# A mixture of experts from dense products to routed tiles of 128 rows, in a four-layer decoder kernel

## The chip, the cores and the metric

The kernel runs on one core of one Trainium2 chip. The metric is the time of one execution on the device, in microseconds. The core has TensorE (PE), VectorE (DVE), ScalarE (ACT), GpSimd (Pool), SyncE (SP, here a queue of transfers) and 16 DMA engines. All of them read their own instruction stream in order and wait for each other by semaphores.

## What is computed

A decoder with four layers on x of 4 batches x 256 tokens x 128 features, float32. Each layer adds a self-attention, a cross-attention to a context of 4 x 512 x 128, and a feed-forward part. Layer 0's feed-forward part is the one that changes:

```python
def _L0_ffn_ref(x, w_router, W1, b1, W2, b2, Ws1, bs1, Ws2, bs2):   # x = layernorm of the stream
    D_MODEL, D_FF, N_EXPERTS, TOP_K, N_SHARED = (128, 512, 8, 2, 1)
    SCALE = 1.0 / math.sqrt(N_SHARED + TOP_K / N_EXPERTS)
    logits = jnp.einsum('btd,ed->bte', x, w_router)
    probs = jax.nn.softmax(logits, axis=-1)
    vals, idx = jax.lax.top_k(probs, TOP_K)
    gates = jnp.sum(jax.nn.one_hot(idx, N_EXPERTS, dtype=x.dtype) * vals[..., None], axis=-2)
    hs = jax.nn.gelu(jnp.einsum('btd,fd->btf', x, Ws1) + bs1)
    acc = jnp.einsum('btf,df->btd', hs, Ws2) + bs2
    h = jax.nn.gelu(jnp.einsum('btd,efd->btef', x, W1) + b1)
    y = jnp.einsum('btef,edf->bted', h, W2) + b2
    acc = acc + jnp.einsum('bted,bte->btd', y, gates)
    return SCALE * acc
```

Every token has two chosen experts of eight, and a shared expert beside them. Layers 1 to 3 follow; layer 1 begins with an attention in hyperbolic form (`L1a`).

## The kernel before

It is one fully unrolled program: each engine has a Python function that writes its instructions in order, and the functions walk the same list of steps. Tokens are eight tiles of 128 (`NT`), tile t with its tokens on the partitions; `x` holds the stream, `xn` the normalised tokens, `xnT` the same turned, features on the partitions. A group g is four tiles, two batches of 256.

Cross-attention of layer 0 (`X0`) runs in slots (`cross_slot`); a slot up to 63 makes scores, slots 20 to 83 exponentials, and the last batch closes up to slot 95. Slot 66 holds the router's products for group 0 (`route`), DVE follows with `route_first` and `route_rest`, which find the two highest of eight. From slot 86 on the mixture's first products stand between the slots (`GELU_BEFORE`).

The mixture (`l0_mixture`) is dense. A unit u is a pair of group and expert, 9 experts (eight and the shared one) x 2 groups. For each unit PE makes four up-projections (`gelu_up`, 128 hidden rows x 512 tokens each, into the banks h0 and h1 in turn), ACT applies gelu with the bias of the hidden row (`gelu`), PE makes 16 down-projections per unit (`down`, four hidden parts for each of four token tiles, into banks e0 and e1), and DVE adds the result times the gate to x (`add_down`; an expert that isn't chosen has gate 0). The weights of all nine experts lie in `ffn_w`, 4.6 MB, loaded long before. Ups run two units ahead of downs. The gated sum of the biases b2 comes from `turn_gates` and `gated_bias`.

While group 1 is in the mixture, group 0 already enters layer 1: `l1_early(q)`, q from 0 to 35, are small pieces (norm turned, projection, the hyperbolic map on DVE with square root and exponentials on ACT, rows turned, query and key parts through DRAM into the stacks, then the nearest products `l1_near` and `l1_roots` of the first two units). Two of them stand at every half unit of group 1. After the mixture `l1_attention` goes on with batches 2 and 3 (`l1_take`) and eight units.

Pool makes the last step of each norm (`root`), and splits and sums of the attentions; SP issues nearly all transfers in one order (`self_attention_inputs` writes query and key parts and reads them back as stacks). An SP wait stops all transfers behind it.

Of the kernel before, what the change touches and what calls it, by code (L numbers as in the profile page):

```python
# [31 lines left out]
P = 128  # L32
# [21 lines left out]
NE = 8  # L54
# [8 lines left out]
HALF_STEPS = float(3 << 21)  # L63
BELOW_ONE = 1.0 - 2.0 ** -23
# [137 lines left out]
F2_HID0 = 108  # L202
F2_UP0 = 144
# [39 lines left out]
def build(nc, d, out, ctx):  # L243
# [44 lines left out]
    cm = sb("cm", [P, NT])  # L288

# [30 lines left out]
    def rows_by_head(tile):  # L320
# [22 lines left out]
                for part in (ffn_w[:, ROOM_AT + 3072:ROOM_AT + 5120], wk(4096, 2048))]  # L343
# [13 lines left out]
    pts[X1] = pts[X2] = pts[X0]  # L357
    gatesT = parts[:].rearrange("p s t -> p (s t)").bitcast(F32)[0:NE + 1, 0:TOK]
# [13 lines left out]
    v_scr = nc.dram_tensor("v_scr", (P, NC * VA), F32)  # L372

    (d_x, d_ident, d_keep, d_l0a, d_ctx, d_bf, d_rows, d_b2, d_ones, d_mrow, d_raw,
     d_cwrite, d_kxwrite, d_lam, d_cfill, d_vload, d_mask3, d_w, d_w1, d_w2, d_w3, d_out) = (
        semaphore("dma_" + n) for n in (
            "x", "ident", "keep", "l0a", "ctx", "bf", "rows", "b2", "ones", "mrow", "raw",
            "cwrite", "kxwrite", "lam", "cfill", "vload", "mask3", "w", "w1", "w2", "w3", "out"))
# [17 lines left out]
    rope_k, mask_row, vx_set = semaphore("rope_k"), semaphore("mask_row"), semaphore("vx_set")  # L396
    ctx_ps, ctx_done, gram_ps, gram_done, ctx_bias, c_split, kx_split, far_done, farT_ps, farT_done = (
        semaphore(n) for n in ("ctx_ps", "ctx_done", "gram_ps", "gram_done", "ctx_bias", "c_split", "kx_split",
# [13 lines left out]
    l1_pool_sq = semaphore("l1_pool_squared")  # L412
# [5 lines left out]
    UP0, HID0, DOWN0, BIAS0 = ({"L0f": 0, "L1f": 72, "L3f": 0}, {"L0f": 0, "L1f": 72, "L3f": 0},  # L418
                               {"L0f": 0, "L1f": 36, "L3f": 36 + L1F_UNITS}, {"L0f": 0, "L3f": 2})
    EXPERTS = {"L0f": NE + 1, "L1f": NE + 1, "L3f": NE}  # L420
    ROUTE_AT = {"L0f": 1, "L1f": 3, "L3f": 5}
    UPS, HIDS = {"L0f": up_ps, "L1f": up_ps, "L3f": up3_ps}, {"L0f": hidden, "L1f": hidden, "L3f": hidden3}

    def w1_of(st, e, j):
        if st == "L0f":
            return ffn_w[:, (e * FJ + j) * P:(e * FJ + j + 1) * P]
        if e < L3F_OWN:
            return ffn_w[:, (e * FJ + j) * P:(e * FJ + j + 1) * P]
        return ctx_flat[:, ((e - L3F_OWN) * FJ + j) * P:((e - L3F_OWN) * FJ + j + 1) * P]

    def w2_of(st, e, j):
        at = (e * FJ + j) * E
        if st == "L0f":
            return ffn_w[:, 9 * FH + at:9 * FH + at + E]
# [11 lines left out]
    def x_ready(st, b):  # L446
        if st == "L0a":
            return d_x, 16
        if st in ("L1a", "L2a"):
            ffn = "L0f" if st == "L1a" else "L1f"  # L450
            return down_x, down_at(ffn, EXPERTS[ffn] - 1, b)
        before = {"L0x": "L0a", "L0f": "L0x", "L1x": "L1a", "L1f": "L1x", "L2x": "L2a", "L2f": "L2x",
                  "L3a": "L2f", "L3x": "L3a", "L3f": "L3x"}[st]
        return x_done, X_AT[before, b]

# [38 lines left out]
    def route_tmp(i):  # L494
        flat = parts[:].rearrange("p s t -> p (s t)").bitcast(F32)
        return flat[:, TOK + i * NT * NE:TOK + (i + 1) * NT * NE].rearrange("p (t e) -> p t e", e=NE)

# [38 lines left out]
    def tensor_program():  # L536
# [304 lines left out]
        def turn_gates(st, n, g, routed):  # L841
            pe.wait_ge(gated, routed)
            claim("e1")
            for i in range(4):
                m = pe.transpose(ps_e[1][0:n, i * P:(i + 1) * P], gates[:, 4 * g + i, 0:n], ident)
            m.then_inc(gate_ps, 1)
            free["e1"] = (gate_T, BIAS0[st] + g + 1)

        def gated_bias(st, which, n, g):
            count = BIAS0[st] + g + 1  # L850
            claim("e0")
            pe.wait_ge(gate_T, count)
            for i in range(4):
                t = 4 * g + i
                m = pe.matmul(ps_e[0][:, i * P:(i + 1) * P], gatesT[0:n, t * P:(t + 1) * P], b2[0:n, which, :],
                              start=True, stop=True)
            m.then_inc(bias_ps, 1)
            free["e0"] = (bias_x, count)
# [23 lines left out]

        def l0_mixture():
            n_exp = NE + 1
            done = 0
            for t in range(TAILX, LAST[X0]):
                if t == min(GELU_BEFORE):
# [2233 lines left out]
```

## Time and profile before

| | |
|---|---|
| median of 3 runs | 1241.89 us (1233.96 to 1242.09) |
| span of the profiled execution | 1242.7 us |
| its difference to the median | 0.8 us more |
| instructions | 19890 |
| PE busy | 1039.3 us (84%) |
| DVE busy | 795.0 us (64%) |
| ACT busy | 611.8 us (49%) |
| Pool busy | 252.3 us (20%) |

The span runs from the first instruction to the last of one execution; no other time of that execution is known. Busy times are sums over stages with different limits, so a share says little about one stage: what matters is which engine is full in the stretch that a change touches, and what the others wait for there. A matmul in float32 shows as two records on PE, each with its own weight load (PEld). The granted clock is that of TensorE as a part of 2.4 GHz.

### The profile page before, as it was taken

The page shows a single profiled execution, that of the slowest core. Times are in us where ns is not written, and L with a number is a line of the kernel's source. Part 1 is how long each engine was busy: PE and PEld are TensorE (multiplying, and loading weights), DVE is VectorE, ACT ScalarE, POOL GpSimd, SP SyncE. Part 2 cuts the span into 40 slices and gives each one's busy share as a digit, 9 for nine tenths or more (in the row PEclk, how much of TensorE's full clock was granted, in tenths as well). Part 3 has the DMA queues.
Part 4 walks back from the last instruction along what each step waited for, and adds up shares of the span by engine and source line. Part 5 has one row for each costly group of instructions (what it writes and reads, how often), then busy time and mean ns, then how long its engine had stood idle before and what let it go on. Part 6 is the DMA issues. An engine that isn't in the chain of part 4 may idle for free.

```text
span 1242.7 us, 19890 instructions
## 1 busy us (share of the span) xinstructions
PE 1039.3 (84%) x7649; PEld 556.7 (45%) x7649; DVE 795.0 (64%) x1984; ACT 611.8 (49%) x1018; POOL 252.3 (20%) x309
## 2 busy tenths in 40 slices
PE   5777699999899975788877889999658878869999
PEld 4233223333677652355542333566323334437757
DVE  7786867731315468887767883777687886575412
ACT  2456356666334437678753777323125555333342
POOL 2933400000000225577641000001131001000000
PEclk9789879999999986566765999999867888779999
DMA  8332140000000300077014202600102100000000
GB/s 303 95 89 69 39 167 2 2 2 1 1 1 1 102 35 1 1 216 143 1 45 141 101 2 36 109 1 3 49 26 72 59 1 2 34 1 1 1 9 9
DMA packets 34786, 61.25 MB, mean 49 GB/s; under 512 B 4771, under 2 KB 25076, under 8 KB 33092
## 3 DMA queue, kind: packets, MB, share of 16 engines
q1 hardware_dynamic: 33828, 58.64, 16.5%
q8 instruction: 62, 1.02, 0.3%
q10 hardware_dynamic: 864, 1.33, 0.3%
q14 instruction: 32, 0.26, 0.1%
HBM read 42.91 MB, written 16.65 MB: 48 GB/s over the span
## 4 chain that ended last, share of the span: by engine, by line
PE 62%; DVE 27%; ACT 5%; issue 4%; DMA 1%; POOL 1%; SPq 0%; DVEq 0%; ACTq 0%; POOLq 0%
PE ps_s L879 10%; PE ps_e L869 9%; PE ps_v L672 7%; DVE mx L1864 5%; PE ps_e L608 5%; PE ps_s L629 3%; PE ps_e L606 3%; PE ps_e L973 2%; DVE ps_s L1860 2%; DVE mx L1854 2%; PE ps_s L960 2%; ACT work L1396 2%; PE ps_s L1124 1%; PE ps_v L1144 1%; DVE work L2339 1%
## 5 line engine op out<-in xcount | busy, mean ns | idle before, releaser
L1396 ACT ACTIVATE work<-ps_e 128x512 f32<-128x512 f32 x448 | 250.7, 598 | 144.3 <-PE ps_e L608 139.1
L2618 POOL TENSOR_TENSOR rstd<-rstd,halves 128x2 f32<-128x2 f32 x52 | 36.6, 705 | 699.5 <-DVE rstd L1807 699.4
L1864 DVE TENSOR_REDUCE mx<-ps_s 128x2 f32<-128x1024 f32 x128 | 154.0, 1222 | 30.0 <-PE ps_s L629 28.5
L629 PE MATMUL ps_s<-ctx_stack,q_stack 49*128 49x512 bf16 (+1 forms) x384 | 129.0, 452 | 46.0 <-DVE mx L1864 33.7
L1498 ACT ACTIVATE work<-ps_s,keep 128x512 f32<-128x512 f32 x136 | 93.0, 687 | 140.3 <-PE ps_s L879 137.3
L608 PE MATMUL ps_e<-q_stack,ctx_stack 52*128 52x256 bf16 (+1 forms) x768 | 151.4, 298 | 9.1 <-ACT work L1396 3.6
L672 PE MATMUL ps_v<-work,vaug 128*32 128x256 f32 x1536 | 132.4, 421 | 4.6 <-ACT work L1384 4.6
L869 PEld LDWEIGHTS ps_e<-ffn_w,work 128*128 128x128 f32 x960 | 118.9, 197 | 21.6 <-issue 20.5
L879 PE MATMUL ps_s<-xnT,ffn_w 128*128 128x512 f32 x240 | 118.4, 617 | 3.6 <-ACT work L1498 3.6
L869 PE MATMUL ps_e<-ffn_w,work 128*128 128x128 f32 x960 | 120.7, 281 | 0.8 <-DVE x L2050 0.8
L2060 DVE SCALAR_TENSOR_TENSOR x<-ps_e,gates,x 128x128 f32<-128x128 f32 x128 | 38.9, 346 | 123.4 <-PE ps_e L869 120.3
L1860 DVE CUSTOM_DVE_ANT_0 ps_s<-ps_s,work 128x512 f32<-128x512 f32 x128 | 86.0, 717 | 29.1 <-PE ps_s L629 29.1
L608 PEld LDWEIGHTS ps_e<-q_stack,ctx_stack 52*128 52x128 bf16 (+1 forms) x768 | 45.0, 97 | 105.2 <-ACT work L1396 49.5
L629 PEld LDWEIGHTS ps_s<-ctx_stack,q_stack 49*128 49x128 bf16 (+1 forms) x384 | 29.6, 97 | 72.2 <-DVE mx L1864 46.7
L879 PEld LDWEIGHTS ps_s<-xnT,ffn_w 128*128 128x128 f32 x240 | 41.7, 195 | 41.9 <-issue 25.3
L672 PEld LDWEIGHTS ps_v<-work,vaug 128*32 128x32 f32 x1536 | 31.7, 112 | 49.8 <-issue 36.7
L606 PE MATMUL ps_e<-work,ident_b 128*128 128x512 bf16 x128 | 51.8, 404 | 2.3 <-issue 2.3
L2677 POOL TENSOR_TENSOR work<-work 128x1536 f32<-128x1536 f32 x14 | 47.9, 3441 | 0.9 <-ACT work L1642 0.8
L1376 ACT ACTIVATE xnT<-ps_m 128x256 f32<-128x256 f32 x36 | 13.7, 382 | 61.9 <-PE ps_m L554 60.1
L1854 DVE TENSOR_REDUCE mx<-ps_s 128x4 f32<-128x1024 f32 x32 | 38.1, 1220 | 9.4 <-PE ps_s L624 9.1
L1895 DVE RECIPROCAL rsum<-ps_s 128x8 f32<-128x8 f32 x48 | 9.7, 203 | 48.9 <-PE ps_s L577 48.7
L577 PE MATMUL ps_s<-keep,work 128*128 128x128 f32 x128 | 29.3, 312 | 12.9 <-ACT work L1384 6.5
(379 smaller groups left out, 1821.5 us busy)
## 6 DMA issues: line engine op xcount, KB each, us to landing
q_stack<-q_scr SPq DMA_DIRECT2D x32, 192.0 KB
ffn_w<-in_L0f_w SPq DMA_DIRECT2D x1, 4608.0 KB, 15.9
ffn_w<-in_L1f_w SPq DMA_DIRECT2D x1, 3456.0 KB, 12.9
q_scr<-parts SPq DMA_DIRECT2D x16, 192.0 KB, 2.1
c_scr<-ffn_w SPq DMA_DIRECT2D x12, 256.0 KB, 7.1
kx_scr<-ffn_w SPq DMA_DIRECT2D x12, 256.0 KB, 4.1
ctx_stack<-kx_scr SPq DMA_DIRECT2D x2, 1536.0 KB
ctx_stack<-c_scr SPq DMA_DIRECT2D x2, 1536.0 KB
```

What stands on the lines that cost most here:

```text
L606: pe.matmul(bank[name], ident_b[:], far_k[:, b, k:k + 2, :].rearrange("p k q -> p (k q)"), start=True, stop=False, skip_group_check=True)
L608: m = pe.matmul(bank[name][:, half * S:(half + 1) * S], stack[p0:p0 + n_rows, pair, k * P:(k + 1) * P], q_stack[p0:p0 + n_rows, b, pair, : ...
L629: return pe.matmul(ps_s[i][:, parity, :], q_stack[p0:p0 + n_rows, b, pair, part * P:(part + 1) * P], ctx_stack[p0:p0 + n_rows, pair, b * S ...
L672: m = pe.matmul(ps_v[j * COLS:(j + 1) * COLS, 0:S], values(b * nkt + k, g % 4 * GROUP + j), pt[:, j % 2, k % 2, :], start=(k == 0), stop=( ...
L869: m = pe.matmul(bank[name][:, i * P:(i + 1) * P], hid[:, j, (t0 + i) * P:(t0 + i + 1) * P], w2(e, j), start=(j == 0), stop=(j == FJ - 1))
L879: pe.matmul(bank[name], w1_of(st, e, j), xnT[:, g * 512:(g + 1) * 512], start=True, stop=True).then_inc(UPS[st], 1)
L1396: act.activation(pt[:, parity, :, :].rearrange("p k q -> p (k q)"), bank[f"e{parity}"], ACT.Exp).then_inc(exped, 1)
L1498: act.activation(hid_unit(st, u)[:, j, :], bank[f"h{n % 2}"], ACT.Gelu_apprx_tanh, bias=b1).then_inc(HIDS[st], 1)
L1854: m = dve.tensor_reduce(mx[:, b, :, pair, :], ps_s[i][:].rearrange("p a (q k) -> p a q k", q=TPB), AX, ALU.max, negate=True)
L1860: m = dve.tensor_tensor_reduce(ps_s[i][:, parity, :], ps_s[i][:, parity, :], far_q[:, b * TPB + part, :], 1.0, -3e38, ALU.add, ALU.max, mx ...
L1864: m = dve.tensor_reduce(mx[:, b, :, pair, part], ps_s[i][:], AX, ALU.max, negate=True)
L2677: pool.tensor_tensor(c, c, l1_s[:, HALVES[n], :], ALU.add).then_inc(added, 1)
```

## The change

The dense mixture of layer 0 becomes a routed one.

- For each group of 512 tokens DVE takes the two chosen experts per token (`chosen`); PE counts with small products how many tokens come before each within an expert (`moe_rank`: a triangular matrix of 2^66 and a vector of it). DVE turns the counts into a row number for both choices of every token, each expert beginning at a multiple of 128, and from the same counts the expert of each tile of 128 rows (`moe_place`). 1024 rows with 8 experts fill at most 15 tiles; 15 are always computed (`SPARSE_TILES`).
- Pool scatters the 1024 rows to DRAM with eight indirect transfers per group (`send_rows`); SP loads them back in order (`rows_in`); PE turns the 15 tiles (`moe_turn`) and DVE copies them to `xgT`.
- 38 tile steps follow: 15 of group 0, 8 of all tokens with the shared expert, 15 of group 1. Each has four up-projections and four down-projections of 128 columns (`tile_rise`, `tile_fall`). The start column of each tile's expert is loaded into registers of PE and DVE (`moe_experts`, 15 registers each per group). DVE copies the expert's W1 into a ring of four buffers (`stage`), addressed by register; PE reads W2 in place, addressed by register. ACT makes four gelus of 128 columns per tile with biases picked by `moe_place`.
- The routed results go by groups of four tiles to SBUF (ACT), to DRAM (a store issued by ACT, `y_group`), and are fetched per token by eight indirect gathers per group on Pool (`take_y`). DVE adds them times the gate (`add_chosen`). The shared expert's results are added from PSUM (`add_shared`).
- The 36 early pieces of layer 1 stand at other places: 22 of them two to a tile in the last eleven tiles, 14 after the last tile.
- Beside that: DRAM scratch for both groups is filled once with rows of x by four transfers (so that unused rows hold numbers), the gate and bias products use banks m and v, and several semaphores are reused.

The diff, cut to its core:

```diff
-GELU_FIRST = [(u, j) for u in range(3) for j in range(FJ)]
-GELU_BEFORE = {87: 1, 88: 1, 89: 2, 90: 2, 91: 2, 92: 2, 93: 2}
 ROUTE0 = 66
-GATES1 = 3
+SPARSE_TILES = (2 * 4 * P + NE * (P - 1)) // P
+MOE_TILES = [(0, i) for i in range(SPARSE_TILES)] + [("all", t) for t in range(NT)] + [(1, i) for i in range(SPARSE_TILES)]
+MOE_BEFORE = {86: 1, 87: 1, 88: 1, 89: 1, 90: 1, 91: 1, 92: 1, 93: 1}
+MOE_RANK0, MOE_PLACE0, MOE_TURN0 = 69, 70, (82, 83, 84, 85)
+MOE_RANK1, MOE_GATES1, MOE_TURN1 = 10, 12, (21, 22, 24, 26)
+MOE_MIX0 = (25, 26)
+MOE_EARLY = {n: (2 * (n - 27), 2 * (n - 27) + 1) for n in range(27, 38)}
+MOE_RING = 4
...
+        def moe_experts(st, g):
+            pe.wait_ge(*planned(st, g, "experts"))
+            _, at = nc.values_load_multi_w_load_instructions(
+                expert_at[0:1, g, 0:SPARSE_TILES], engines=[mybir.EngineType.PE], min_val=0, max_val=(NE - 1) * FH,
...
+        def tile_rise(n):
...
+                pe.wait_ge(xg_T, XG_T0 + 4 * g + i // 4 + 1)
+                pe.wait_ge(staged, STAGED0 + MOE_STAGED.index(n) + 1)
+            for j in range(FJ):
+                if g == "all":
+                    w = ffn_w[:, (NE * FJ + j) * P:(NE * FJ + j + 1) * P]
+                else:
+                    w = w1_staged[MOE_STAGED.index(n) % MOE_RING][:, j * P:(j + 1) * P]
+                m = pe.matmul(bank[name][:, j * P:(j + 1) * P], w, rhs, start=True, stop=True)
+            m.then_inc(tile_up, 1)
+            free[name] = (tile_hidden, n + 1)
+
+        def tile_fall(n):
...
+            pe.wait_ge(tile_hidden, n + 1)
+            for j in range(FJ):
+                lo = 9 * FH + j * E
+                w = ffn_w[:, lo + NE * FH:lo + NE * FH + E] if g == "all" else ffn_w[:, bass.ds(expert_of[g][i] + lo, E)]
+                m = pe.matmul(bank[name][:, at:at + P], tile_hid[n % MOE_RING][:, j, :], w, start=j == 0, stop=j == FJ - 1)
+            m.then_inc(tile_down, 1)
+            free[name] = moe_group_done(k)
+
+        def moe_step(n):
...
+            if n in MOE_TURN1:
+                moe_turn(1, MOE_TURN1.index(n))
+            if n + 2 < len(MOE_TILES):
+                tile_rise(n + 2)
+            if n == MOE_STAGED[SPARSE_TILES]:
+                moe_experts("L0f", 1)
+            tile_fall(n)
+            for q in MOE_EARLY.get(n, ()):
+                l1_early(q)
...
+            for n in range(n, len(MOE_TILES)):
+                moe_step(n)
+            for q in range(2 * len(MOE_EARLY), 36):
+                l1_early(q)
...
+        def tile_gelu(n):
...
+            act.wait_ge(tile_up, n + 1)
+            for j in range(FJ):
+                bias = kp("L0f_bs1", j, 1) if g == "all" else hidden_bias[g][:, i * FJ + j:i * FJ + j + 1]
+                m = act.activation(tile_hid[n % MOE_RING][:, j, :], bank[moe_tile_bank(n)][:, j * P:(j + 1) * P],
+                                   ACT.Gelu_apprx_tanh, bias=bias)
+            m.then_inc(tile_hidden, 1)
...
+        def stage(n):
+            m = MOE_STAGED.index(n)
+            g, i = MOE_TILES[n]
+            if m >= MOE_RING:
+                dve.wait_ge(tile_up, MOE_STAGED[m - MOE_RING] + 1)
+            dve.tensor_copy(w1_staged[m % MOE_RING], ffn_w[:, bass.ds(expert_of[g][i], FH)]).then_inc(staged, 1)
...
+        def add_chosen(b):
+            g = b // 2
+            dve.wait_ge(moe_x, g + 1)
+            dve.wait_ge(d_y_own[b % 2], 64 * (g + 1))
+            for c in range(2):
+                for t in tiles(b):
+                    m = dve.scalar_tensor_tensor(x[:, t, :], y_own[g][:, t % 4, c, :], chosen_gate[:, c, t:t + 1],
+                                                 x[:, t, :], ALU.mult, ALU.add)
...
+        def send_rows(st, g):
...
+            pool.wait_ge(*planned(st, g, "placed"))
+            for c in range(2):
+                for t in range(4 * g, 4 * g + 4):
+                    pool.indirect_dma_start(rows_scr[g].ap()[:, :], bass.IndirectOffsetOnAxis(ap=place_of[:, c, t:t + 1], axis=0),
+                                            xn[:, t, :], None).then_inc(d_rows_out, 16)
+
+        def take_y(st, g):
+            pool.wait_ge(d_y_out[g], Y_OUT0[g] + 64)
+            for b in (2 * g, 2 * g + 1):
+                for t in tiles(b):
+                    for c in range(2):
+                        pool.indirect_dma_start(y_own[g][:, t % 4, c, :], None, y_scr[g].ap()[:, :],
+                                                bass.IndirectOffsetOnAxis(ap=place_of[:, c, t:t + 1], axis=0)
+                                                ).then_inc(d_y_own[b % 2], 16)
...
+        def rows_in(g):
+            sp.wait_ge(d_rows_out, 128 * (g + 1))
+            sp.dma_start(xg[g], rows_scr[g].rearrange("(t p) f -> p t f", p=P)).then_inc(d_rows_in, 16)
```

## Rows read from the trace of the kernel before

**Rows 1.** The page, 40 equal slices of the span, PE's busy tenths.

```profile
PE   5777699999899975788877889999658878869999
```

**Rows 2.** The page, the chain that ended last, shares of the span by engine.

```profile
PE 62%; DVE 27%; ACT 5%; issue 4%; DMA 1%; POOL 1%; SPq 0%; DVEq 0%; ACTq 0%; POOLq 0%
```

**Rows 3.** Busy time in stretches: PE, PEld, DVE, ACT, Pool, clock, DMA share, GB/s.

```profile
316.60:380.00 63.40, 61.69 (x345) 46.07 (x346) 14.65 (x55) 21.79 (x31) 0.00 (x0) 0.95 0.00 1
380.00:427.00 47.00, 45.35 (x256) 32.61 (x255) 25.45 (x82) 23.52 (x39) 9.44 (x18) 1.00 0.13 40
```

**Rows 4.** Timeline (start, length): first up, first down, a load, last down.

```profile
296.39 1.12 PE L879 MATMUL ps_s<-xnT,ffn_w 128*128 128x512 f32 x2
...
316.65 5.39 PE L869 MATMUL ps_e<-ffn_w,work 128*128 128x128 f32 x32 [0.78 <-DVE x L2050]
...
323.17 0.19 PEld L869 LDWEIGHTS ps_e<-ffn_w,work 128*128 128x128 f32 x1 [0.24 <-issue]
...
454.99 2.00 PE L869 MATMUL ps_e<-ffn_w,work 128*128 128x128 f32 x16
```

**Rows 5.** The chain that ended last, in order of time: start, length, what.

```profile
369.32 1.72 PE ps_s L879 x4
371.04 1.78 PE ps_e L869 x16
...
449.39 3.16 PE ps_e L869 x16
```

**Rows 6.** Timeline of the attention's end: last gate operation, exponentials, two transposes.

```profile
266.24 0.19 DVE L2038 TENSOR_TENSOR gates<-parts 128x32 f32<-128x32 f32 x1
...
290.92 1.24 ACT L1396 ACTIVATE work<-ps_e 128x512 f32<-128x512 f32 x2 [0.61 <-PE ps_e L608]
...
311.61 0.38 PE L554 MATMUL ps_m<-keep,xn 128*128 128x128 f32 x2
```

**Rows 7.** Groups of instructions by form: count, busy us, mean ns, idle before.

```profile
L2627 POOL TENSOR_TENSOR x<-x,rows 128x128 f32<-128x128 f32 x32 | 12.8, 421 | 10.3 <-DVE xn L1820 10.3
L2677 POOL TENSOR_TENSOR work<-work 128x1536 f32<-128x1536 f32 x14 | 47.9, 3441 | 0.9 <-ACT work L1642 0.8
L2020 DVE TENSOR_TENSOR parts<-parts 128x32 f32<-128x32 f32 x12 | 2.3, 193 | 0.4
L1860 DVE DVE_READ_ACCUMULATOR2_ANT mx<- 128x1 f32 x128 | 18.1, 141 | 0.0
L1498 ACT ACTIVATE work<-ps_s,keep 128x512 f32<-128x512 f32 x136 | 93.0, 687 | 140.3 <-PE ps_s L879 137.3
L1606 ACT ACTIVATE ctx_stack<-ctx_stack 128x128 f32<-128x128 f32 x2 | 0.6, 309 | 3.4 <-DVE ctx_stack L2258 3.4
L2237 DVE TENSOR_SCALAR work<-work 128x256 f32<-128x256 f32 x4 | 1.2, 289 | 0.1
L2237 DVE TENSOR_SCALAR work<-work 128x704 f32<-128x704 f32 x4 | 2.1, 527 | 0.1
L2239 DVE TENSOR_TENSOR work<-work 128x704 f32<-128x704 f32 x4 | 3.6, 893 | 0.1
```

**Rows 8.** DMA issues: times, KB each, median us from issue to landing.

```profile
q_scr<-parts SPq DMA_DIRECT2D x16, 192.0 KB, 2.1
```

**Rows 9.** Timeline of layer 1's start, first `l1_take` to the last two.

```profile
388.39 0.96 DVE L2311 TENSOR_TENSOR ctx_stack<-ps_s,rows 128x770 f32<-128x770 f32 x1 [0.69 <-PE ps_s L1060]
...
415.38 0.56 DVE L1830 TENSOR_TENSOR parts<-qT,parts 128x256 bf16<-128x256 f32 x1
415.97 1.46 SPq L2805 DMA_DIRECT2D q_scr<-parts  x3
...
427.61 0.34 PE L1073 MATMUL ps_s<-self_stack,q_stack 48*128 48x128 bf16 x4
...
458.77 0.68 DVE L2319 TENSOR_REDUCE mx<-ps_s 128x2 f32<-128x512 f32 x1
...
465.16 0.96 DVE L2311 TENSOR_TENSOR work<-ps_s,rows 128x770 f32<-128x770 f32 x1 [3.41 <-PE ps_s L1060]
```

More of the change, by code:

```diff
@@ L881, in gelu_up, with moe_rank @@
             free[name] = (HIDS[st], n + 1)
+        def moe_rank(st, g, name):
+            claim(name)
+            pe.wait_ge(*planned(st, g, "counted"))
+            ps = bank[name]
+            ones = ones_big[:].broadcast_to([P, P])
+            pe.matmul(ps[:, 0:4 * NE], far_b[:], chosen[:].rearrange("p t e -> p (t e)"), start=True, stop=False,
+                      skip_group_check=True)
+            for i in range(3):
+                pe.matmul(ps[:, (i + 1) * NE:4 * NE].rearrange("p (t e) -> p t e", e=NE), ones,
+                          chosen[:, i:i + 1, :].broadcast_to([P, 3 - i, NE]), start=False, stop=i == 2,
+                          skip_group_check=True)
+            for i in range(4):
+                m = pe.matmul(ps[:, 4 * NE:5 * NE], ones, chosen[:, i, :], start=i == 0, stop=i == 3,
+                              skip_group_check=True)
+            m.then_inc(ranked, 1)
+            free[name] = planned(st, g, "placed")
@@ L1501, in l0_mixture, with moe_step @@
+        def moe_step(n):
+            if n == -1:
+                tile_gelu(0)
+                tile_gelu(1)
+                return
+            if n + 2 < len(MOE_TILES):
+                tile_gelu(n + 2)
+            k = MOE_GROUP_OF[n]
+            if n == MOE_GROUPS[k][-1] and MOE_TILES[n][0] != "all":
+                y_group(k)
+            for q in MOE_EARLY.get(n, ()):
+                l1_early(q)
         def l0_mixture():
-            n_exp = NE + 1
-            done = 0
+            n = -1
@@ L1522, in l3_route @@
+            for q in range(2 * len(MOE_EARLY), 36):
+                l1_early(q)
         def l3_route(g):
@@ new lines, in moe_turn, with moe_experts @@
+        def moe_turn(g, k):
+            lo, hi = 4 * k * P, min(4 * k + 4, SPARSE_TILES) * P
+            if k == 0:
+                dve.wait_ge(*planned("L0f", g, "biases"))
+            dve.wait_ge(xg_ps, XG_PS0 + 4 * g + k + 1)
+            dve.tensor_copy(xgT[g][:, lo:hi], bank[moe_turn_bank(g, k)][:, 0:hi - lo]).then_inc(xg_T, 1)
+        def moe_experts(st, g):
+            dve.wait_ge(*planned(st, g, "experts"))
+            _, at = nc.values_load_multi_w_load_instructions(
+                expert_at[0:1, g, 0:SPARSE_TILES], engines=[mybir.EngineType.DVE], min_val=0, max_val=(NE - 1) * FH,
+                skip_runtime_bounds_check_because="the vector engine clamps it to the last expert")
+            expert_of[g] = at
@@ L2780, in gpsimd_program @@
         settle(pool.tensor_tensor(rw("L2a_bin"), rw("L2a_bin"), rw("L2a_gamma"), ALU.mult))
-        for b in range(B):
-            root("L0f", b)
+        root("L0f", 0)
+        root("L0f", 1)
+        send_rows("L0f", 0)
+        root("L0f", 2)
+        root("L0f", 3)
+        send_rows("L0f", 1)
+        take_y("L0f", 0)
         l1_attention()
@@ L2969, in sync_program @@
         sp.wait_ge(down_ps, down_at("L1f", NE, B - 1))
[L2970 removed]
+        sp.dma_start(ffn_w[:, 0:own], d["L3f_w"][:, 0:own]).then_inc(d_w1, 16)
         max_rows(X2, 2)
```

398 lines of the change are left out of this document (287 added, 111 removed).

## Prediction, made before the changed kernel ran

> **What bounds the kernel now.** I read the page first: PE is busy in nearly every slice [rows 1], and the chain that ended last runs through PE for 62% [rows 2]. The stretches around the change came next, with a granted clock of 0.95 and 1.00 [rows 3]. The dense mixture is PE's from 296.4 us, its first up-projection, to 457.0, where its last down-projection ends [rows 4]: PE is busy 61.7 of 63.4 us in the first half while ACT has 21.8 and DVE 14.7. From 380 the second half of the mixture runs beside the first steps of the next layer (`l1_early`), and PE still stays near full.
>
> The chain shows the pattern that a reader should keep: 1.72 us for two up-projections of 512 columns, 1.78 us for eight down-projections of 128, over and over [rows 5]. So an up costs 0.86 us and a 128-column matmul 0.223 us; at half clock eight cost 3.16 us.
>
> **Experts on PE.** Before: 18 units (nine experts, two groups) of 4 ups and 16 downs, 2 x (1.72 + 1.78) = 7.0 us each, 126 us. After: 38 tiles of 128 rows (15 per group, always, whatever the routing, and 8 for the shared expert) of 8 matmuls of 128 columns, 1.78 us each, 68 us. That is -58 us on an engine that sets the end. It is the only large credit; all else is a debit.
>
> **In front of the mixture.** The first group is planned inside the attention's last slots. DVE is nearly idle there and PE is full. DVE's gates are done at 266.4 us [rows 6]; one exponential step takes about 2 us of PE, so slot 69 begins near 266, and `moe_rank` may wait 1 us for `chosen`. Its 8 small matmuls cost about 1 us and the 15 transposes 2.3 us (0.11 to 0.19 each, from two in 0.38 [rows 6]). PE is the bound here, so all of it counts: +4.5 us. The ten short operations of `moe_place` ahead of the scatters take about 2.4 us (0.19 each and a gap), those behind 2.6 us [rows 7], and both lie in DVE's idle time.
>
> The eight scatters on Pool, then one load, must be done when slot 82 transposes, near 291 us [rows 6]. From 270.5 that leaves 20 us; less about 2.5 us for each landing (2.1 us for a small store [rows 8]) 15 remain, 1.8 us per scatter. No row shows an indirect transfer: the nearest are Pool's operation on 128x128 (0.42 us) and on 128x1536 (3.43 us) [rows 7]. I take 1.3 us, nearer the first because a scatter has 128 short pieces to describe, and then nothing waits; at 3.4 us this place alone would stall PE by 13 us.
>
> **Registers.** PE and DVE each load 15 start columns per group. No row has a register load; the nearest is DVE's read of an accumulator, 0.14 us [rows 7], hence 2.1 us per set, with ends of 0 and 0.5 us each (an issue on SP [rows 9]), 7.5 us per set. Exposed are DVE's first set (PE's first tile waits for it and for one staging copy) and both of PE's: +6.7 us. The first tiles also stand in the attention's tail: 16 half tiles of 0.89 are 14.3 us where 12 ups were 10.3. That moves work and is no cost by itself.
>
> The Trainium skill, Runtime: NRT & Kernel Launch, section on instruction fetch mechanics, gives about 200 ns per register for such loads, from HBM. By it a set would be 3 us and the sum 2.7 us worse; no run here shows it yet.
>
> **Per tile on the other engines.** ACT: a gelu of 512 columns takes 0.687 us with its per-row bias [rows 7], where a pair of exponentials of 512 without one takes 1.24 [rows 6]; a 128-column pass takes 0.309 us [rows 7]. So 128 columns with bias cost some 0.36, and back to back, as in that pair, down to 0.26. Four are 1.1 to 1.5 us, a quarter of a group's copy, wait and store issue 0.3: 1.4 to 1.8 us against PE's 1.78. It is hidden, barely; at its upper end it costs nothing, but 0.1 us more per tile would cost 4 us. DVE: the staging copy of 512 columns interpolates to 0.43 us between two one-input operations on SBUF, 0.289 for 256 columns and 0.527 for 704 [rows 7]. Hidden, and four tiles ahead.
>
> These one-input operations run at about twice the rate of the two-input ones (0.527 against 0.893 us for 704 columns [rows 7]). The Trainium skill, SBUF — State Buffer, Who interferes with whom, says that such a copy locks Pool out of the port by which it writes descriptors. It speaks against this change, whose staging copies run beside its scatters and gathers: each transfer would be held up to one copy, 0.43 us, and 1.3 would become 1.7. The sum above has room for that.
>
> **The second group.** Rank and 15 transposes +4 us on PE; gates and bias now sit in other banks than the tiles, so PE no longer waits for the addition to x before going on (-1). Scatters begin with `placed` near tile 11, the load must land by tile 21, about 21 us: 2 us per scatter are allowed. The gathers of group 0 follow on Pool and have till tile 25. Behind a late `add_chosen(0)` on DVE stand the staging copies, so lateness would stop PE.
>
> Without the next layer the sum is -58 + 4.5 + 6.7 + 4 - 1 = -44 us.
>
> **What the next layer gives back.** It is the step that a sum of PE time misses. In the kernel before 36 early pieces spread over 66 us of group 1. Now 22 of them stand two to a tile in the last 11 tiles (20 us of PE) and 14 behind the mixture. They form a chain through DVE, ACT with table loads, Pool and DMA. By my clock: before, the expert part of PE from its first down is at 316.65 us; after, tile 7 begins near 327. Twenty tiles (35.6), rank, gates, transposes and PE's registers (about 8.5) bring tile 27 to 371 and the first `l1_take` to 375, where before it was at 388.4. From there [rows 9]:
> - take to the end of the split: 27.6 us before, less three additions of downs (1.8), 25.7 -> 400.7;
> - to the first near product: 11.7 us before (two chained DMA steps with their issues), about 10 -> 410.7. PE has finished its tiles by 408, so these transfers lie bare;
> - 7 near and 4 root pieces up to the last reduction: 31.8 us before, with eight groups of downs between; without them PE 0.7, DVE 1.05 and 0.3 of hand-over per near, 2.35 per root, 23.5, plus 2 us because PE's clock may fall when its tiles are gone (it was half from 449 on [rows 5]) -> 436.2;
> - to the last `l1_take`: 5.7 us before; now two `add_chosen` and two norms, 3.8 us each, and 2.8 -> 446.6.
>
> The last gathers (store 3, eight gathers 10.4, landing 2 after the last tile at 408) are done at 423 and hidden behind the 14 pieces; uncovered they would cost 13. That take stood at 465.2 us [rows 9], so the layer starts 18.5 us earlier: of 44 us saved 25 are given back. The remaining layers are unchanged; the renamed semaphores and the 2 MB that fill the scratch rows early (DMA is near idle once the attention's slots have begun) cost nothing.
>
> Sum: 1242.7 - 18.5 = 1224.2 us by the profiled span. The median of the runs is 0.8 us lower than the span, so 1224 us. The three runs differ by 0.65%; 1%, 12.4 us, is about what a measurement here can tell from no change.
>
> **Rivals.**
> 1. PE pays for register-addressed matmuls. Each routed fall has four matmuls (eight records) whose moving operand is at a register, with an addition to form the address. In the trace PE's loads stand idle up to 0.24 us "issue" ahead of a group [rows 4]. If each such matmul costs that much more, a fall costs 0.96 more, 30 of them 29 us, some 5 hidden in the last tiles: 1248 us. Per record it would be 58 us, about 1270: slower. It decides from 0.14 us per record on, where the 18.5 and the 12.4 us are both used up. For it: a tile already has 32 PE instructions in 1.78 us. Against: at full clock those groups run at the pace of the data (0.11 us per record, and 0.2 at half clock [rows 5]), so the queue is not what binds now. The Trainium skill, TensorE: Matmul & The Clock Gate, Part 2, gives about 62 ns per matmul for one decoded in software; by it a record would still fit in 0.11 us, though not with two register additions.
> 2. Indirect transfers are slow, 2.5 us or more each. Group 0 waits 5.6 us, group 1 4, the gathers 5 and the tail 5, so 1224 + 18 = 1242 us: no change. Pool is one queue, and `l1_added_least` stands behind the last eight gathers.
> 3. The chain is looser than it looks: early pieces overlap as before, register loads cost nothing, 1205 to 1213 us. For it: DVE is busy only 25.5 of 47 us in that stretch [rows 3].
> 4. The change doesn't do what it says: 15 tiles always run, where 1024 rows fill 8 to 15; that is already counted.
>
> **How the numbers follow.** Forecast case (1212 to 1230) 0.40; rival 3 0.13; rival 1 in its lighter form 0.12, in its heavy form 0.15; rival 2 0.14; register loads or ACT's cadence at their upper ends (1230 to 1245) 0.06. Likeliest: 1224 us. Its own range is 1212 to 1234, from the 23.5 us piece (up to 31.8) and from faster hand-overs. For 8 in 10: 1205 to 1260. Faster by over 1% (below 1229.5): 0.48; within 1%: 0.27; slower (above 1254.3): 0.25.
>
> **What would show it.** Tiles of 1.8 us with PE full from tile 7 to 27; an attention tail 4 to 5 us longer; idle PE of 10 us or more around the first near product; the `l1_take` of the last batch near 447 us. Wrong if falls are visibly longer than rises, if PE waits for DVE's staging, if Pool's queue is solid from the first scatter on, or if PE's clock is half inside the tiles.

## The result, and the profile after

| | us | runs |
|---|---|---|
| before | 1242.4 (1233.5 to 1249.1) | 20 |
| after | 1248.3 (1240.7 to 1254.7) | 20 |
| forecast | 1224 (1205 to 1260) | |

The ratio is 1.005, 95% interval 1.0029 to 1.0072: slightly slower, where I had forecast 1.5% faster. The profiled execution of after took 1250.0 us, its span is 1248.3 (before: 1242.7). The time lies inside my range, but by luck: rival 1's 1248 is the nearest figure that I named, and its mechanism isn't what happened. The repeats below make the story unusual: on two other chips the same program took 1223.7 and 1227.6, on a third 1248.6.

First the page of after, PE's busy tenths and its granted clock by slice of 31.2 us, to be held against [rows 1].

```profile
PE   6777699999898524778877989999658868779999
PEclk9789879995888856556775999999867989879999
```

The clock of before by the same slices, and its windows around the tail of the attention (stretch, length, busy time of PE, PE's loads, DVE, ACT and GpSimd, then granted clock, DMA share and GB/s):

```profile
PEclk9789879999999986566765999999867888779999
```

```profile
280.00:290.00 10.00, 10.00 (x80) 3.36 (x76) 1.37 (x6) 6.67 (x13) 0.67 (x1) 1.00 0.01 2
290.00:300.00 10.00, 8.64 (x74) 2.67 (x66) 0.43 (x2) 5.87 (x10) 0.00 (x0) 1.00 0.01 2
300.00:310.00 10.00, 8.56 (x25) 3.67 (x26) 1.76 (x8) 5.39 (x10) 0.36 (x1) 1.00 0.00 0
```

The tiles themselves are what I priced. Two pieces of the chain that ended last (start, length, what), the rise (four up-projections) of one tile and the fall (four down-projections) of an earlier one:

```profile
327.80 0.89 PE ps_s L999 x8
328.69 0.89 PE ps_e L1013 x8
```

A fall takes its weights from an address in a register, the rise here from a fixed one, and both take 0.89 us, as the 1.78 us for sixteen records in [rows 5] promised. PE's busy time went from 1039.3 to 999.7 us, and to 985.9 in the same program on chip 6. So the gain is there, and it is lost elsewhere. These milestones say where (start times in us; "unchanged, chip 6" is the same program, experiment r1):

| | before | forecast | after | unchanged, chip 6 |
|---|---|---|---|---|
| first work of the experts on PE | 296.4 | 301 | 317.6 | 301.1 |
| first `l1_take` | 388.4 | 375 | 400.0 | 375.8 |
| first near product | 427.6 | 410.7 | 433.4 | 409.1 |
| third `l1_take` | 465.2 | 446.6 | 474.1 | 447.7 |
| end of the span | 1242.7 | 1224.2 | 1248.3 | 1227.2 |

Most of the loss is there before the first tile. The windows show why, with the columns of those above. Both fences are the attention's last slots, first after, then the same program on chip 6:

```profile
285.00:310.00 25.00, 25.00 (x113) 6.48 (x110) 2.06 (x7) 9.12 (x16) 0.12 (x1) 0.50 0.11 31
```

```profile
285.00:310.00 25.00, 20.20 (x170) 10.91 (x168) 5.79 (x14) 13.13 (x31) 0.00 (x0) 1.00 0.05 13
```

PE is full in after and does less: 113 matmul records where the other has 170. Its clock is at 1.2 GHz (0.50) through the tail, where it was 1.00 before the change (the windows of before above). What happened just before it fell is in the timeline of after:

```profile
277.55 0.44 PE L650 MATMUL ps_m<-keep,xn 128*128 128x128 f32 x2
...
279.10 0.64 PE L737 MATMUL ps_v<-work,vaug 128*32 128x256 f32 x8
279.14 0.96 POOL L3005 DMA_INDIRECT rows_scr<-xn,l0a_ss  x1 [0.30 <-issue]
279.90 0.38 ACT L1537 ACTIVATE qT<-ps_m 128x256 f32<-128x256 f32 x1 [2.21 <-remote]
...
280.40 0.96 POOL L3005 DMA_INDIRECT rows_scr<-xn,l0a_ss  x1 [0.30 <-issue]
280.43 0.68 PE L658 MATMUL ps_s<-keep,qT 128*128 128x128 f32 x4 [0.68 <-issue]
281.31 0.60 ACT L1545 ACTIVATE work<-ps_e 128x512 f32<-128x512 f32 x1 [1.03 <-issue]
...
281.96 0.39 PE L671 MATMUL ps_e<-work,ident_b 128*128 128x512 bf16 x1 [0.85 <-issue]
...
282.65 0.39 SPq L3191 DMA_DIRECT2D self_stack<-rows_scr  x1
...
282.88 0.42 DVE L2114 TENSOR_TENSOR x<-ps_s,x 128x256 f32<-128x256 f32 x1 [8.36 <-remote]
...
283.38 0.39 PE L671 MATMUL ps_e<-work,ident_b 128*128 128x512 bf16 x1 [0.71 <-ACT work L1545]
...
284.24 1.08 PE L737 MATMUL ps_v<-work,vaug 128*32 128x256 f32 x8
```

ACT needs only L650, which ended at 277.99, and starts at 279.90, 1.9 us late; DVE needs L658, over at 281.11, and starts at 282.88, 1.8 us late. The trace can tie neither start to an engine's signal ("remote"), so whether the signal or the engine itself is held isn't shown. PE has three gaps, 0.68, 0.85 and 0.71 us, and the clock falls behind the last: L737 takes 0.64 us at 279.10 and 1.08 at 284.24. All this falls beside the last two of the eight scatters and in the 2 us behind them. On chip 6 the same two instructions start 0.03 us after theirs:

```profile
276.21 0.44 PE L650 MATMUL ps_m<-keep,xn 128*128 128x128 f32 x2
...
276.68 0.38 ACT L1537 ACTIVATE qT<-ps_m 128x256 f32<-128x256 f32 x1 [0.34 <-PE ps_m L650]
...
278.33 0.71 PE L658 MATMUL ps_s<-keep,qT 128*128 128x128 f32 x4
...
279.07 0.42 DVE L2114 TENSOR_TENSOR x<-ps_s,x 128x256 f32<-128x256 f32 x1 [5.90 <-PE ps_s L658]
```

The same picture returns in after beside the gathers of group 0. DVE's copy needs the transposes that ended at 376.79 and starts 3.5 us later; PE waits 4.24 us for it, and its clock is down afterwards (0.70 over 380 to 390).

```profile
376.19 0.60 PE L973 MATMUL ps_v<-keep,ctx_stack 128*128 128x128 f32 x4
...
380.25 0.69 DVE L2262 COPY work<-ps_v 128x512 f32<-128x512 f32 x1 [4.20 <-remote]
380.58 0.94 POOL L3013 DMA_INDIRECT self_stack<-y_scr,l0a_ss  x1 [0.31 <-issue]
...
381.04 1.19 PE L999 MATMUL ps_s<-work 128*128 128x128 f32 x4 [4.24 <-issue]
```

### The profile page after: what moved, and what is told of

It reads as the page before. It is cut to its first block, busy times and chain, and to the rows that moved or that the text cites. A ratio compares the mean times of both kernels' runs of the same rounds, so it can differ in the third digit from the quotient of the medians.

```text
span 1248.3 us, 20081 instructions
## 1 busy us (share of the span) xinstructions
PE 999.7 (80%) x7583; PEld 543.1 (44%) x7583; DVE 806.5 (65%) x2007; ACT 609.0 (49%) x1106; POOL 284.2 (23%) x341
## 3 DMA queue, kind: packets, MB, share of 16 engines
q0 software_dynamic: 1024, 2.10, 0.6%
## 4 chain that ended last, share of the span: by engine, by line
PE 57%; DVE 29%; ACT 6%; issue 5%; DMA 2%; POOL 1%; SPq 0%; DVEq 0%; ACTq 0%; POOLq 0%
PE ps_v L737 7%; DVE mx L2040 6%; PE ps_e L673 5%; PE ps_s L946 5%; PE ps_e L936 4%; PE ps_s L694 3%; PE ps_e L671 3%; PE ps_s L999 3%; PE ps_e L1118 2%; DVE ps_s L2036 2%; DVE mx L2030 2%; PE ps_s L1105 2%; ACT work L1545 2%; PE ps_e L1013 2%; DVE work L2626 1%
## 5 line engine op out<-in xcount | busy, mean ns | idle before, releaser
L737 PE MATMUL ps_v<-work,vaug 128*32 128x256 f32 x1536 | 134.6, 427 | 4.3 <-ACT work L1533 4.3
L1644 ACT ACTIVATE work<-ps_s,keep 128x512 f32<-128x512 f32 x64 | 43.8, 687 | 68.0 <-PE ps_s L946 66.6
L2318 DVE SCALAR_TENSOR_TENSOR x<-ps_e,gates,x 128x128 f32<-128x128 f32 x64 | 19.4, 346 | 60.9 <-PE ps_e L936 58.0
L671 PE MATMUL ps_e<-work,ident_b 128*128 128x512 bf16 x128 | 55.0, 430 | 3.8 <-issue 3.1
L737 PEld LDWEIGHTS ps_v<-work,vaug 128*32 128x32 f32 x1536 | 31.8, 113 | 49.6 <-issue 35.6
L946 PE MATMUL ps_s<-xnT,ffn_w 128*128 128x512 f32 x96 | 50.8, 659 | 2.0 <-ACT work L1644 2.0
L1656 ACT ACTIVATE work<-ps_s,kv 128x128 f32<-128x128 f32 x120 | 34.0, 370 | 33.9 <-PE ps_s L999 33.8
L936 PEld LDWEIGHTS ps_e<-ffn_w,work 128*128 128x128 f32 x384 | 46.0, 192 | 7.8 <-issue 7.7
L936 PE MATMUL ps_e<-ffn_w,work 128*128 128x128 f32 x384 | 46.4, 275 | 0.0
L619 PE MATMUL ps_m<-keep,xn 128*128 128x128 f32 x80 | 19.8, 336 | 29.9 <-DVE xn L1996 28.4
L1013 PE MATMUL ps_e<-ffn_w,work 128*128 (+1 forms) x304 | 43.6, 291 | 0.0
```

The source lines that it names most:

```text
L671: pe.matmul(bank[name], ident_b[:], far_k[:, b, k:k + 2, :].rearrange("p k q -> p (k q)"), start=True, stop=False, skip_group_check=True)
L737: m = pe.matmul(ps_v[j * COLS:(j + 1) * COLS, 0:S], values(b * nkt + k, g % 4 * GROUP + j), pt[:, j % 2, k % 2, :], start=(k == 0), stop=( ...
L936: m = pe.matmul(bank[name][:, i * P:(i + 1) * P], hid[:, j, (t0 + i) * P:(t0 + i + 1) * P], w2(e, j), start=(j == 0), stop=(j == FJ - 1))
L946: pe.matmul(bank[name], w1_of(st, e, j), xnT[:, g * 512:(g + 1) * 512], start=True, stop=True).then_inc(UPS[st], 1)
L1013: m = pe.matmul(bank[name][:, at:at + P], tile_hid[n % MOE_RING][:, j, :], w, start=j == 0, stop=j == FJ - 1)
```

## Experiments

Theory 1: the indirect transfers hold up the other engines for some 2 to 4 us, PE idles, and its clock falls. The edits are against after. e1, e2, e9, e10, e12, e13 and e14 leave out the sorting of the rows by expert, and e4 the choice of the expert, so these eight don't compute the mixture; the number and size of their tiles are those of after.

**1. What carries the rows (e1, e2; chip 4).** `send_rows` and `take_y` (in e2 `send_rows` alone) leave GpSimd; SP sends plain transfers of the same size:

```diff
-        send_rows("L0f", 0)
-        send_rows("L0f", 1)
-        take_y("L0f", 0)
...
+                for t in range(4 * g, 4 * g + 4):
+                    lo = (4 * c + t % 4) * P
+                    sp.dma_start(rows_scr[g].ap()[lo:lo + P, :], xn[:, t, :]).then_inc(d_rows_out, 16)
```

> All 32 indirect transfers are replaced by plain transfers of the same bytes, pieces and semaphore counts from SP's queue, so tokens are not sorted by expert (that part of the computation is left out; tiles, weights, registers and adds stay). Theory 1 (the indirect transfers hold up PE, ACT and DVE for 1 to 3 us each time they run, PE's granted clock then falls to 1.2 GHz and stays there through the exponential tail): the clock stays 1.00 from 280 to 312, the first tile starts at 304 to 307 instead of 317.6, the stall at 377 to 381 is gone, and the kernel takes 1222 to 1232. Theory 2 (the clock falls because the ranking matmuls, the transposes and their waits were put into PE's order in the slots, whatever carries the rows): the clock falls at 283 as after, time 1244 to 1250.

> Only the 16 scatters are plain transfers from SP's queue; the 16 gathers stay indirect on GpSimd (rows are not sorted by expert, as said of the run with all 32). Theory 1: the clock's fall at 283 is gone with the scatters, the tail of the exponentials runs at 1.00, first tile at 304 to 307, but the stall at 377 beside the gathers and the odd waits at 433 to 441 stay; 1228 to 1238. Theory 2: as after, 1244 to 1250. If the time is that of the run with all 32 plain, the gathers cost nothing.

Measured: 1225.3 (ratio 0.984, interval 0.979 to 0.990) and 1221.0 (0.982, 0.977 to 0.987), clock 1.00 from 285 to 310 in both. e2 is below its own range of 1228 to 1238: the gathers cost nothing there. The rest looks like theory 1, until the next two are read.

**2. The wait for the gates, and the registers (e3, e4; chip 4).**

```diff
-MOE_RANK1, MOE_GATES1, MOE_TURN1 = 10, 12, (21, 22, 24, 26)
+MOE_RANK1, MOE_GATES1, MOE_TURN1 = 10, 14, (21, 22, 24, 26)
```

```diff
-            _, at = nc.values_load_multi_w_load_instructions(
...
+            expert_of[g] = [i // 2 * FH for i in range(SPARSE_TILES)]
```

> The second group's gate transposes and bias stand at step 14 instead of 12, so DVE has finished placing the second group before PE waits for its copy. Theory 1 counts this wait (354.8 to 357.3) and the half clock behind it (358 to 362) as 4 to 5 us that nothing later absorbs: 1242 to 1245. Rival (the path behind the mixture is set by the second group's scatters, their landing and the transposes, not by PE): the wait goes, but the last fall stays at 424 to 426 and the time at 1247 to 1249.

> The expert of each tile is a constant of the program (tile i takes expert i/2), no registers are loaded and no address is taken from one: the choice of the expert is left out, all else stays. My term of 2.1 us for a set of register loads: both sets shown as 1.8 us on DVE, of which the first is exposed, so 1 to 3 us less: 1245 to 1247. Rival 1 of the prediction (register-addressed matmuls are slow): falls shorter than 0.89 us and 15 or more us off the time, 1233 or less. The trace of after speaks against that: falls take 0.89 us, as the rises with fixed addresses do.

Measured: 1222.7 (0.986, 0.980 to 0.992) and 1221.9 (0.986, 0.981 to 0.990). e3 is 20 us below all that was expected of it and differs from after only from 350 us on, long after the damage. e4's time would suit rival 1 (1233 or less), but its falls, now with fixed addresses, take the same 0.89 us; by its other term it is 23 us too low. A result that no theory allows is a reason to repeat the base, not to explain.

**3. The unchanged kernel again, and two that barely differ (chip 6).** e5 has the gates at step 13, e6 one more memset at the start.

> The changed kernel once more, unchanged, on the chip of these runs. The run with the gates two steps later took 1222.7 although its program and its work are the same as after up to 350 us, and it shows none of after's stalls at 278 to 283. Theory 3 (the stalls beside the scatters belong to this program as it is loaded, or to its exact order): 1245 to 1252, with the scatters landing in a median of some 6 us and the first tile at 317. Theory 4 (they belonged to the runs shown, not to the kernel): about 1226 to 1229, the gates' move being worth 4 to 6 us.

> Second group's gates and bias at step 13 instead of 12 (14 took 1222.7). Up to 350 us nothing differs from after in what is computed or in its order. Theory 3 by the order behind 350: PE still waits a little for DVE here, and the time lies between 1223 and 1230. If the program's placement decides and not the order, the stalls at 278 to 283 may be back and the time 1240 to 1248.

> After with one memset of GpSimd more at the very start of the program (it writes a constant a second time, some 0.1 us where GpSimd is free), so that only the placement of GpSimd's instructions differs. Theory 3 by placement: the stalls at 278 to 283 go and the time falls to 1226 to 1230. Theory 3 by order: 1245 to 1252 as after. Theory 4: the same as the repeated after, whatever that is.

Measured: 1227.6 (0.987, 0.980 to 0.993), 1227.2 and 1224.5, all at a clock of 0.93 to 1.00 over 285 to 310, with no "remote" wait in it. Theory 4 (the stalls belonged to the runs shown, not to the kernel): neither order nor placement matters. One reading of mine has to be taken back here and in all expectations that repeat it: the "6.1 us" was the landing of other transfers to the same tensor. Of the scatters in after the trace shows no landing. They are not late: SP, which waits for all eight, issues its load 1.29 us after the last scatter's issue ended in after (281.36 to 282.65), and 1.28 us in r1 (280.02 to 281.30).

**4. A third repeat and an idle made by hand (chip 15).**

```diff
+            if t == OVERLAP + 75:
+                pe.wait_ge(d_rows_out, 128)
```

> The changed kernel unchanged, a third time. Repeated on another chip than that of the first experiments it took 1227.6, its scatters landed in a median of 2.2 us (6.1 us in the profile after) and its tail of exponentials ran at a granted clock of 1.00. If slow landings come with the chip or its state and not with the kernel, this one is either such a chip (landings of 6 us, half clock from 283 on, 1245 to 1252) or not (2.2 us, 1.00, 1224 to 1230); nothing between.

> After, and PE waits behind slot 75 of the cross-attention until the first group's 8 scatters have landed, so that it idles some 3 us at 279 to 282, where the profile after shows its idle. Theory 1, clock part (an idle of 2 to 3 us there takes the granted clock to 1.2 GHz for the whole tail of the exponentials): the clock reads 0.50 from about 283 to 310, the first tile comes 13 to 20 us later than in the unchanged kernel of the same chip, and the time is 12 to 18 us above it. Rival (the idle costs itself only, the clock fell for another reason): clock 1.00, 2 to 4 us more.

> The same wait one slot later, where only 1 to 1.5 us of idle are left. Theory 1: if the clock falls here too, the tail is as sensitive as that, and the time is again 12 to 18 us above the unchanged kernel; if it does not, the idle must be longer than that to cost the clock, and the time is 0 to 2 us above.

> The kernel with the second group's gates at step 14 again, to stand beside the unchanged one on one chip. It took 1222.7 where before took 1242.6, the unchanged one 1227.6 where before took 1243.3. The wait for DVE's copy is 2.0 us and the half clock behind it costs about 2.5 us in the repeated profile: 4 to 5 us below the unchanged one. If other waits absorb it: within 2 us.

Measured: 1248.6 (1.006, 1.003 to 1.009; 10 runs), 1246.9, 1250.2 and 1250.4. This chip does what the result showed: "remote" waits beside the scatters in all four, clock 0.50 to 0.55 over 285 to 310. The added waits change nothing, since PE idles there anyway. e3's kernel took 1222.7 on chip 4 and 1250.4 here, and before took 1242.6 and 1242.0. So the change has two values, by chip: I call chips like 4 and 6 the first sort, those like this one the second. On this chip the move of the gates gains nothing, 1250.4 against 1248.6, where 4 to 5 us were expected. In r1 PE waits for the copied gates, in e3 for a staged expert, which stands behind the same `moe_place(1)` on DVE:

```profile
338.85 1.12 PE L922 MATMUL ps_v<-b,parts 9*128 9x128 f32 x8 [1.99 <-DVE parts L2302]
```

```profile
340.06 1.13 PE L999 MATMUL ps_s<-self_stack,work 128*128 128x128 f32 x8 [1.82 <-DVE work L2276]
...
345.17 1.12 PE L922 MATMUL ps_v<-b,parts 9*128 9x128 f32 x8 [0.86 <-DVE parts L2302]
```

**5. Which transfers, on a chip of the second sort (chip 13).** e9 and e10 are the kernels e1 and e2; e11 is e7; in e12 GpSimd issues the 32 transfers with fixed rows:

```diff
-                    pool.indirect_dma_start(rows_scr[g].ap()[:, :], ...
+                    lo = (4 * c + t % 4) * P
+                    pool.dma_start(rows_scr[g].ap()[lo:lo + P, :], xn[:, t, :]).then_inc(d_rows_out, 16)
```

> All 32 indirect transfers plain from SP's queue (rows not sorted by expert), once more, in the hope of a chip on which the indirect scatters land in 6 us; the run with the wait at slot 75 shows which kind this one is. Theory 5 (on such a chip the software-described transfers hold up the other engines, and the 21 us between 1227.6 and 1248.5 are theirs): 1222 to 1230 whatever the chip. Rival (such a chip is slow for this kernel also without them, by its clock for instance): 1240 to 1250 where the kernel with them has 1248. On a chip with landings of 2.2 us: 1222 to 1230 by both.

> Only the 16 scatters plain, the gathers indirect. Theory 5 on a chip with slow landings: the first group's scatters cost 13 to 16 us by the lost clock of the tail of the exponentials, the gathers the rest: 1228 to 1236, first tile near 301 and clock 1.00 to 300. If the gathers do not matter: as with all plain.

> All 32 transfers issued by GpSimd as direct ones with fixed rows (not sorted by expert): same queue, bytes and pieces as the indirect ones, no row numbers. On a chip with slow landings, theory 5a (it is the software queue that holds the engines up): 1243 to 1250 as with indirect ones. Theory 5b (it is the row by row addressing): 1222 to 1230. On a chip with landings of 2.2 us it tells only what issuing costs GpSimd: within 3 us of the others.

> PE waits behind slot 75 for the first group's scatters to land. On the chip with slow landings it took 1246.9, as the unchanged kernel, whose PE idles there anyway. On a chip with landings of 2.2 us: theory 1's clock part gives a granted clock of 0.50 from about 283 to 310 and 1238 to 1246; without it 1228 to 1232.

| chip 13 | us | ratio, interval |
|---|---|---|
| e11, all indirect (and the wait) | 1251.6 | 1.007, 1.004 to 1.010 |
| e10, gathers indirect | 1234.9 | 0.993, 0.991 to 0.996 |
| e12, none, from GpSimd | 1226.8 | 0.988, 0.984 to 0.991 |
| e9, none, from SP | 1228.3 | 0.986, 0.982 to 0.990 |

This is the answer for such chips. Without indirect transfers the kernel takes there what it takes elsewhere. The gathers cost 6.6 to 8.1 us (e10 against e9 and e12) and the scatters 17, with e11's wait in them. It is not the load of GpSimd's queue alone (theory 5a): e12 sends the same number of packets through it (1024, 2.10 MB). But its eight sends are issued in 4.5 us, where eight scatters take 10.2 in after, so the slower issue and the addressing by row (theory 5b) aren't told apart. In e10 the attention's tail runs at 1.00 and only the gathers' place shows the late starts:

```profile
363.67 1.14 ACT L1656 ACTIVATE work<-ps_s,keep 128x128 f32<-128x128 f32 x4 [4.66 <-remote]
363.83 0.69 DVE L2262 COPY work<-ps_v 128x512 f32<-128x512 f32 x1 [4.35 <-remote]
```

**6. The clock's share, and rows in order (chip 11).** e13 is e12 with PE waiting behind slot 75 until the rows are in; e14 keeps the indirect form and gives it a constant table of rows.

> All 32 transfers direct from GpSimd (fixed rows, not sorted by expert; this took 1226.8 on a chip where the indirect ones land in 6 us), and PE waits behind slot 75 until the first group's rows have come in: an idle of 2.4 us at 280.2 to 282.6, made without any indirect transfer. Theory 1, clock part: the granted clock reads 0.50 from some 284 to 312, the first tile comes 14 to 18 us later than at 302, and the time is 1238 to 1246. Rival (the idle is harmless, the clock fell for what the indirect transfers did besides): clock 1.00, first tile at 304 to 305, 1228 to 1231.

> All transfers stay indirect, but the row numbers that they are given come from a constant table and run in order (row 128*(4c+t)+p for copy c, tile t, partition p); tokens are not sorted by expert. On a chip where the unchanged kernel's scatters land in 6 us: theory 5c (the indirect form costs, whatever the rows) 1244 to 1250 and landings near 6 us; theory 5d (scattered rows cost) 1224 to 1230 and landings near 2.2 us. On a chip with landings of 2.2 us for the unchanged kernel both say 1224 to 1230 and nothing is told apart.

> The changed kernel unchanged, one look, to say which kind of chip this is: scatters landing in 2.2 us and 1224 to 1230, or in 6 us and 1245 to 1252.

The unchanged kernel took 1223.7 in its single run, so this is a chip of the first sort, and e14 (1226.8; 0.987, 0.983 to 0.991) tells nothing apart. e13 does not need the second sort. It took 1240.8 (1.000, 0.997 to 1.003), 14 us above e14 on the same chip, and as much above e12, which ran on chip 13. Its idle, and the window behind it:

```profile
284.81 0.39 PE L671 MATMUL ps_e<-work,ident_b 128*128 128x512 bf16 x1 [2.02 <-DMA self_stack<-rows_scr]
...
286.10 1.04 PE L737 MATMUL ps_v<-work,vaug 128*32 128x256 f32 x8
```

```profile
285.00:310.00 25.00, 24.05 (x110) 6.50 (x111) 2.07 (x7) 9.43 (x17) 0.07 (x1) 0.52 0.00 1
```

An idle of 2.02 us, with no indirect transfer in the kernel, takes the clock to 0.50. The bf16 matmuls right behind it still take 0.39 us each, then those of L737 go from 0.64 to 1.04, and the window is that of after almost line for line. The clock reads 0.50 from 286.2 to 310, 24 us in which PE is busy for 96% of the time, and is back between the first and the second group of transposes.

Profiles differ in where the last gate operation stands (the `gates<-parts` row of [rows 6]), so I count from it:

| us | that operation | to the first tile (before: first up) | to the first `l1_take` | to the end |
|---|---|---|---|---|
| before | 266.24 | 30.15 | 122.15 | 976.5 |
| r1 | 266.04 | 35.02 | 109.78 | 961.2 |
| e12 | 267.27 | 35.02 | 109.85 | 957.1 |
| e13 | 269.80 | 47.31 | 123.05 | 969.9 |
| after | 267.39 | 50.22 | 132.66 | 980.9 |

The one idle costs e13 12.3 us up to the first tile and 12.8 to the end, 14 by the medians. After loses 15.2 us against r1 up to the first tile, so the idle and its clock are most of it, and 7.7 more up to the first take, the stretch with the gathers (e10 loses 5.9 there against e12).

How much an idle costs is not a matter of its length alone. All changed kernels but e4 wait 2.64 to 2.66 us for DVE ahead of the first tile. In r1, r4, e1, e2, e10, e12 and e14 the clock stays at 1.00 behind it, and the first sixteen records take 2.02 us. In e3, e5, e6 and e9 it falls to 0.50 for some 3.5 us and is back, and they take 3.51 to 3.58. Of these idles only those in the tail, in e13 and on chips of the second sort, kept it down for 24 us and more. Why they did is not shown.

```profile
301.06 2.02 PE L999 MATMUL ps_s<-self_stack,work 128*128 128x128 f32 x16 [2.65 <-DVE work L2276]
```

## Why the prediction was wrong

**The step that failed** is the last sentence on the scatters: "I take 1.3 us, nearer the first because a scatter has 128 short pieces to describe, and then nothing waits". The size held. A scatter takes GpSimd 0.96 us and 0.30 to the next, 1.26; a gather 0.94 and 0.30. "Nothing waits" did not. On the chips of the result's sort operations of ACT and DVE that need only a result of PE start 1.8 to 3.5 us late while a batch of eight runs. I priced a transfer only by its own queue (rival 2 as well, at 2.5 us each) and took the attention's tail, where PE was full at 1.00, to bear a hiccup. It couldn't: there 2 us of idle cost 12 to 14 (e13).

**In front of the mixture**, +4.5 us: measured +4.7 on chip 6 (301.1 against 296.4) and +21.2 in after. That the first agrees so well is in part luck: it holds 2.65 us of waiting for DVE, which I had put under registers and staging, and the first tile stands one slot earlier than the first up did.

**Experts on PE**, -58 us: shown by the tile's 0.89 + 0.89. Rival 1 is dead: the falls take that on both sorts of chip, and in e4 with fixed addresses. The addition that forms an address shows as a register operation of 46 ns ahead of each of the 120 routed down-projections, and no fall is longer for it. The Trainium skill's page TensorE: Matmul & The Clock Gate, Part 2, gives about 62 ns per matmul decoded in software; the trace allows it, at 0.11 us per record nothing of it shows.

**Registers**, 2.1 us per set: DVE's load took 1.79 us (0.12 per register), PE's none that shows, since it lies behind the first two rises. In e4 PE's wait ahead of the first tile is 1.08 us where r1 has 2.65, so some 1.6 were exposed, not 6.7. Its total cannot be told from the others. The Trainium skill's page Runtime: NRT & Kernel Launch, on instruction fetch mechanics, says 200 ns per register from HBM. These come from SBUF, and the measured 120 decides.

**ACT and staging.** Four gelus take 1.14 us (forecast 1.1 to 1.5), a staging copy 0.43 as forecast. The copies did stop PE, for 1.82 us at 330 in r1 and twice in e3 (a sign against me on my own list), for a reason I did not list: they stand behind the planning operations on DVE, in whose idle time I had put them. The Trainium skill's page SBUF — State Buffer, Who interferes with whom, would add up to a copy's time to each transfer; beside the four staging copies from 374.52 to 376.04 in after the gathers took 0.95 and 1.08 us where others take 0.94, so at most 0.14 shows there. A scatter of the second group took 1.26 (0.96 otherwise) beside DVE's last planning operations and one copy; which of them did it isn't told apart.

**The next layer** is the part that held best. On chip 6 the first take came at 375.8 (375), the first near at 409.1 (410.7), the last reduction of those pieces at 436.3 (436.2), the third take at 447.7 (446.6), with PE idle for 7.5 of the 11 us ahead of the near product and its clock at 0.50 behind it. There the total is 1227.6, against my 1224, with before at 1243.3: 15.7 us gained of the 18.5 forecast. The signs that I listed were to be seen there, beside PE's wait for staging, and in after the last one on my list of what would refute it: half clock, though ahead of the tiles more than inside them.

**The chances** don't follow from my cases: those above 1254.3 hold 0.15, and "slower" was given 0.25.

**Open.** Why ACT and DVE start late on some chips and not on others; the runs of each numbered set here came from one chip at one time, so chip and hour cannot be parted. Whether scattered rows or the indirect form does it: rows in order were run only on a chip that does not show it. On which chip the result's own runs were taken isn't known; its trace is of the second sort throughout. No version that computes the mixture was found safe on both sorts: e3 takes 1222.7 on one and 1250.4 on the other, and e5 and e6, which took what the unchanged kernel takes on chip 6, ran on no chip of the second sort.

## What to carry to other kernels

Ask of every transfer not only what its queue pays but who else is running full beside it, and don't put a batch of indirect transfers beside the stretch in which PE is the bound. Where PE runs full at the high clock, give an idle of 2 us a range up to what the stretch behind it costs at half clock (here 12 to 14 us; in other places of these kernels 2.65 us of idle cost the clock nothing, or 3.5 us at half). When an edit that can't matter moves the time by 2%, repeat the base on another chip before reading anything into it.

## What the runs showed of the hardware

- One program, two times by chip: 1227.6 and 1223.7 (chips 6, 11) against 1248.6 and 1248.3 us (chip 15 and the result), while the kernel before stays at 1240.6 to 1243.3 on all of them.
- An indirect transfer of 128 rows of 512 bytes takes GpSimd 0.96 us (scatter) or 0.94 (gather) and 0.30 to the next; a direct one of the same size 0.54.
- After an idle of 2.0 us the granted clock was 0.50 for 24 us with PE busy for 96% of them (e13), and for 30 us without a gap in after (283.7 to 314). After 2.65 us ahead of the first tile it stayed at 1.00 in seven profiles and was 0.50 for some 3.5 us in e3, e5, e6 and e9.
- Matmuls with an operand addressed by register ran at the pace of fixed ones, 0.89 us for four, with one register operation of 46 ns for each.
